# New steps for every kind of work in a planned two-stage attention kernel

## Chip, core and metric

The kernel runs on one core of a Trainium2 chip. The metric is the device time of one execution in microseconds, the median of several runs.

## What is computed

x is 8 batches of 1024 rows of 512 channels; ctx is 8 batches of 1024 rows of 384. Two stages follow each other, both in fp32:

```python
# stage 1: cross attention, 8 heads of 64
q = layernorm(x) @ Wq;  k = ctx @ Wk;  v = ctx @ Wv
x = x + tanh(g_xattn) * (softmax(q @ k.T / 8) @ v @ Wo + bo)
# stage 2: self attention, 16 heads of 32, q normalised, gated
y = layernorm(x); q, k, v = (y @ W.T + b for each)
q = (q / |q| + query_embedding) * softplus(temperature)
h = softmax(q @ k.T / sqrt(32)) @ v
gates = softmax(h @ Wr.T + br), only the best 3 of 15 kept, times 3
s = softmax(h @ Ws.T + bs); w = 2 * s
x = x + tanh(g_ffn) * ((h * (w0 * s0 + w1 * sum(gates))) @ Wp.T + bp)
```

## The kernel before

**Tiling.** A batch has 64 steps, counted on through all 16 batches of work (8 of stage 1, then 8 of stage 2). Step T is 128 keys against 512 queries of one group of heads: 2 heads in stage 1, 4 in stage 2. A batch has 4 groups of 16 steps, a half group (8 steps) shares its queries. In a step the tensor engine (PE) makes the scores of each head (kind "S", line 925), ScalarE (ACT) their exponentials ("ex", L1128) into a ring of buffers, PE the weighted values of all heads ("PV", L942), and GpSimd (POOL) adds the exponentials up ("ad", L817), for the sums of the softmax ("sm", L954, made to factors by "sma" and "ev").

**Work that fills.** Around the steps lies the work for later groups and batches. "pq" and "pk" project queries and keys of a group (L839); "sd" copies them by DMA into `stack` as high and low parts. "mx" makes all scores of a head once more (L902) and VectorE (DVE) takes their maxima ("mxr", L1286); "mt", "ml" and "md" turn these and bring them by DMA into `stack`, where the scores read them. "vp" and "vpe" project the values (L839, L1095, L1279). "xl" loads the rows of the next batch, in two halves, "ln", "la", "lb" and "l2" normalise them on DVE and ACT by turns (L1223 to L1242, L1036), "tr", "tra" and "trl" transpose them and split them in high and low (L859, L1043, L1250). "gt" and "gm" make the gates (L963), "hs", "hsl", "op", "ope" and "st" the output (L839, L1349), "xr", "xq" and "xb" bring the residual rows back. "fr" to "fs" split the weights of stage 2 during stage 1, "cx" and "cxl" the context.

**The planner.** Every instruction sequence of every engine is made from one order of about 17,000 items, made by `Plan` when the kernel is built. Each item has an engine, a time, a list of items it comes after, and a step. `Plan.run` keeps its own clock: an engine that is free takes, of the items whose predecessors are done, the one with the lowest step. The steps come from the table `AT`, one dictionary for each stage, relative to the batch: `p` and `over` the start of the four groups' projections and over how many steps they spread, `mx0` and `mxn` start and length of a group's maxima, `ctx`, `load`, `norm`, `turned` the context, the loads, the normalisations and the transposes, `out` the output of each half, `xr` the residual's load, `split` the splitting of the weights; `off` adds a number to all items of one kind. The scores of step T have step T - 1, PV has T + 0.9. The constants of the plan's clock are for instance 0.23 for a score product, 1.05 for PV, 0.52 for an exponential, 1.3 for an addition on POOL, 1.2 for a maximum on DVE; for the normalisation 3.5, 0.5, 0.8 and 3.2; a load is 0.7 on the queue and lands 6 later.

**What is fixed by it.** The order on each queue, and which of the four banks of `aux` a product gets. Each engine takes its instructions strictly in that order and waits with semaphores; the semaphores follow from the order by themselves. The transposes of a batch come, by their list `used`, behind the projections of the last group of the batch before; "S" of a group's first step comes behind "md" of its head; "sd" of the next group comes behind the last score of the group that used the same half of `stack`.

Of the kernel before, what the change touches and what calls it, by code (L numbers as in the profile page):

```python
# [37 lines left out]
class Phase:  # L38


    def __init__(self, ffn):
# [10 lines left out]
        self.SUM = 32 if ffn else 64  # L52
        self.AT = AT[ffn]
        self.first = B if ffn else 0
# [52 lines left out]
    def copied(self, g, e):  # L107
# [1 line left out]
        return g // 2 + 1 if e < PHASES[0].G else (g - NG * B) // 2 + 1  # L109


AT = (dict(p=[2.5, 18.6, 35.2, 51.9], over=7.4, mx0=3, mxn=3, ctx=[-3.6, 18.6, 24.7, 31.5], load=[5.4, 36.9], norm=[10, 28.5],
           turned=[20.8, 34.5], out=[63.1, 58.9], xr=43, split=39, off={}),
      dict(p=[2, 18.6, 36, 50], over=6.5, mx0=0.4, mxn=9, load=[4, 27], norm=[8, 29], turned=[25, 36.6], out=[61, 67], xr=49, off={}))


PHASES = Phase(False), Phase(True)
# [2 lines left out]
def stage(j):  # L120

    return PHASES[j >= B]
# [9 lines left out]
def batch(it):  # L132

    return it[1] // BATCH_HAS[it[0]] if it[0] in BATCH_HAS else 0


class Plan:
# [18 lines left out]
    def add(self, item, engine, time, step, after=()):  # L156

        assert item not in self.work, item
        self.work[item] = (engine, time, after)
        self.step[item] = step + stage(batch(item)).AT["off"].get(item[0], 0)  # L160

    def weights(self):
# [8 lines left out]
        for c in range(4 * NG):  # L171
            j, at = c // NG, c // NG * TURN + PHASES[0].AT["split"] + 3 * (c % NG)
            self.add(("fr", c), "sp", 0.7, at, [("fl", c - 2), ("tr", j + 1, 1, NG - 1)])
# [20 lines left out]
    def attend(self, j):  # L194

        ph, G = stage(j), stage(j).G
        for T in range(TURN * j, TURN * (j + 1)):
# [23 lines left out]
            if jt == TT - 1:  # L221
                b = T + 1 + ph.AT.get("sums", 0)
                self.add(("cp", h), "act", 0.6, T + 0.95, [("PV", T), ("cp", h - 1)])
# [4 lines left out]
    def project(self, g):  # L228
# [3 lines left out]
        source = lambda kind, n: ("cxl", j, 2) if kind == "pk" and not ph.ffn else ("trl", j, n, NG - 1)  # L232
        at, over = ph.AT["p"][(g + 2) % NG] + (g - 2) // NG * TURN, ph.AT["over"]
        self.add(("wl", g), "sp", 2.4, at - 3, [("pk", g - 1, 1, last_g.chunks("pk") - 1), ("pq", g - 1, 1, NG - 1)] + [("ws", i) for i in range(2)] + [("fs", 4 * NG - 1)] * ph.ffn)
# [25 lines left out]
    def maxima(self, g):  # L260

        ph = stage(g // NG)
        last_g = stage((g - 1) // NG)
        step, each = (g - 1) * STEPS + ph.AT["mx0"], ph.AT["mxn"] / ph.G
        for e in range(ph.G):
# [1127 lines left out]
```

## Time and profile before

| | us |
|---|---|
| runs | 5066.6, 5065.87, 5042.02 |
| median | 5065.87 |
| span of the profiled execution, first to last instruction | 5051.8 |
| PE / DVE / ACT / POOL busy | 94% / 58% / 51% / 67% |

The profile page gives busy time for each engine and groups of instructions by line. Records of products overlap each other: a product's record lasts longer than the time after which the next one can follow, so PE can be "busy" and still be held up. The profile has the span of one execution; its device time is not listed by itself, the median of the runs is 14.1 us more than the span.

### The profile page before, as it was taken

How to read it: one execution, taken by the hardware profiler on the slowest of the kernel's cores; microseconds unless marked ns; L12 is line 12 of the kernel's file. 1: busy time of each engine (PE TensorE's matmuls, PEld its weight loads, DVE VectorE, ACT ScalarE, POOL GpSimd, SP SyncE). 2: the span in 40 equal slices, each digit the busy share in tenths (PEclk: the TensorE clock that was granted, in tenths of full speed). 3: DMA queues.
4: the chain of work that ended last, by engine and by line, in shares of the span. 5: the costliest groups of instructions: out<-in, count | busy, mean ns of one | idle time of the engine just before them, and what ended most of it. 6: DMA issues, size and time to landing. Idle time of an engine off the chain costs nothing.

```text
span 5051.8 us, 67410 instructions
## 1 busy us (share of the span) xinstructions
PE 4766.1 (94%) x21696; PEld 2731.3 (54%) x21696; DVE 2946.6 (58%) x4019; ACT 2601.4 (51%) x4705; POOL 3367.3 (67%) x2667
## 2 busy tenths in 40 slices
PE   4999999999999999998998999999999999999997
PEld 3555555556565556564564554554654644645644
DVE  4454545454545454566766656757656666666563
ACT  2444445353535354536636646546556556466454
POOL 1656656574756565747848858767578588578587
PEclk7999999999999999999999999999999999999998
DMA  7343535344343434333233132322323322332320
GB/s 239 97 130 113 129 112 125 117 123 125 97 134 88 142 88 133 93 88 86 57 100 76 45 110 64 84 84 63 94 70 76 93 62 64 92 82 53 101 51 26
DMA packets 285210, 481.11 MB, mean 95 GB/s; under 512 B 32832, under 2 KB 165440, under 8 KB 275648
## 3 DMA queue, kind: packets, MB, share of 16 engines
q1 hardware_dynamic: 284864, 476.79, 34.6%
q8 instruction: 181, 2.97, 0.3%
q14 instruction: 165, 1.35, 0.1%
HBM read 223.14 MB, written 50.33 MB: 54 GB/s over the span
## 4 chain that ended last, share of the span: by engine, by line
PE 50%; DVE 5%; issue 3%; ACT 2%; POOL 1%; SPq 1%; DMA 0%; ACTq 0%; POOLq 0%; DVEq 0%
PE aux L839 15%; PE acc L942 10%; PE aux L902 10%; PE scores L925 9%; DVE nm L1286 4%; PE aux L954 2%; PE aux L963 1%; PE aux L883 1%; POOL added_f L817 1%; PE aux L859 1%; SPq L734 1%; ACT probs L1128 1%; DMA stack<-ck_lo 0%; PE aux L911 0%; DVE st L1223 0%
## 5 line engine op out<-in xcount | busy, mean ns | idle before, releaser
L1286 DVE TENSOR_REDUCE nm<-aux 128x1 f32<-128x1024 f32 x1536 | 1844.7, 1221 | 1192.8 <-PE aux L902 1190.0
L817 POOL TENSOR_TENSOR added<-added,probs 128x512 f32<-128x512 f32 x1433 | 1804.4, 1297 | 856.7 <-PE acc L942 653.4
L1128 ACT ACTIVATE probs<-scores 128x512 f32<-128x512 f32 x2151 | 1189.1, 597 | 862.5 <-PE scores L925 831.3
L925 PE MATMUL scores<-stack 128*128 128x512 f32 x4096 | 1340.3, 417 | 36.3 <-ACT probs L1128 15.8
L902 PE MATMUL aux<-stack 96*128 96x512 f32 (+1 forms) x3072 | 1017.5, 420 | 94.1 <-DVE nm L1286 53.6
L925 PEld LDWEIGHTS scores<-stack 128*128 128x128 f32 x4096 | 735.3, 190 | 639.2 <-ACT probs L1128 223.7
L942 PE MATMUL acc<-probs,vh 128*32 128x512 f32 (+1 forms) x4302 | 968.8, 617 | 20.0 <-ACT vh L1095 20.0
L902 PEld LDWEIGHTS aux<-stack 96*128 96x128 f32 (+1 forms) x3072 | 525.6, 190 | 578.1 <-DVE nm L1286 272.1
L817 POOL TENSOR_TENSOR added_f<-added_f,probs 128x512 f32<-128x512 f32 x537 | 678.9, 1298 | 59.1 <-PE acc L942 36.9
L839 PE MATMUL aux<-xT_hi,wqk 128*128 128x512 f32 x1536 | 580.2, 407 | 13.7 <-ACT qwork L1067 6.9
L1128 ACT ACTIVATE more<-scores 128x512 f32<-128x512 f32 x537 | 300.3, 598 | 155.6 <-PE scores L925 134.7
L804 POOL TENSOR_TENSOR cq_lo<-qwork,cq_hi 128x512 fp32r<-128x512 f32 x64 | 82.5, 1288 | 417.2 <-ACT cq_hi L1083 417.2
L839 PEld LDWEIGHTS aux<-xT_hi,wqk 128*128 128x128 f32 x1536 | 290.3, 189 | 111.7 <-issue 47.6
L942 PEld LDWEIGHTS acc<-probs,vh 128*32 128x32 f32 (+1 forms) x4302 | 156.9, 119 | 303.6 <-issue 221.8
L817 POOL TENSOR_TENSOR added_f<-added_f,more 128x512 f32<-128x512 f32 x231 | 296.0, 1308 | 31.3 <-PE acc L942 25.9
L817 POOL TENSOR_TENSOR added<-added,more 128x512 f32<-128x512 f32 x231 | 291.3, 1292 | 19.4 <-PE acc L942 18.9
L839 PE MATMUL aux<-xT_lo,wqk 128*128 128x512 f32 x768 | 302.7, 394 | 0.0
L942 PE MATMUL acc<-more,vh 128*32 128x512 f32 x1074 | 288.6, 617 | 0.0
L1309 DVE SCALAR_TENSOR_TENSOR aux<-aux,rn 128x512 f32<-128x512 f32 x128 | 88.8, 694 | 249.7 <-ACT rn L1141 234.8
L1128 ACT ACTIVATE added<-scores 128x512 f32<-128x512 f32 x256 | 143.6, 596 | 173.7 <-PE scores L925 170.3
L839 PE MATMUL aux<-wvo,halves_f 128*128 128x512 f32 x768 | 217.6, 426 | 5.9 <-DVE xs L1349 4.4
L823 POOL TENSOR_TENSOR xs<-xs,bo_x 128x512 f32<-128x512 f32 x64 | 81.6, 1289 | 161.5 <-DMA xs<-in_x 161.5
(131 smaller groups left out, 4938.1 us busy)
## 6 DMA issues: line engine op xcount, KB each, us to landing
wqk<-w_split SPq DMA_DIRECT2D x256, 256.0 KB, 3.8
wvo<-w_split SPq DMA_DIRECT2D x64, 1024.0 KB, 6.9
stack<-cq_hi SPq DMA_DIRECT2D x128, 256.0 KB, 5.0
stack<-ck_hi SPq DMA_DIRECT2D x128, 256.0 KB, 4.9
stack<-cq_hi SPq DMA_DIRECT2D x256, 128.0 KB, 2.3
stack<-ck_hi SPq DMA_DIRECT2D x256, 128.0 KB, 2.4
xs<-in_x SPq DMA_DIRECT2D x16, 1024.0 KB, 6.4
stack<-cq_lo SPq DMA_DIRECT2D x64, 256.0 KB, 4.9
```

The lines of the kernel that those rows point to most:

```text
L734: sp.dma_start(stack[row:row + D, g % 2, e * ph.SLOTS + slot, :].bitcast(F32), src[what][half][e * D:(e + 1) * D, :].bitcast(F32)).then_in ...
L804: pool.tensor_tensor(cq["lo"][:, q], qy[:, n], cq["hi"][:, q].bitcast(F32), ALU.subtract).then_inc(qlo_ok, 1)
L817: pool.tensor_tensor(onto, onto, exp_buffer(T, e), ALU.add).then_inc(added_ok, 1)
L823: pool.tensor_tensor(xs[:, t % (TT // 2), :], xs[:, t % (TT // 2), :], bo[:], ALU.add).then_inc(biased, 1)
L839: ins = pe.matmul(out, lhs(a, k), rhs(c, k), start=k == 0 and i == 0, stop=k == whole - 1 and i == 2)
L902: ins = pe.matmul(aux[:, b + j, :], stack[used, g % 2, e * ph.SLOTS + qs, t * P:(t + 1) * P], stack[used, g % 2, e * ph.SLOTS + ks, j * HA ...
L925: ins = pe.matmul(scores[:, u % SCORES, :], stack[:, g % 2, e * ph.SLOTS + ks, jt * P:(jt + 1) * P], stack[:, g % 2, e * ph.SLOTS + qs, n ...
L942: ins = pe.matmul(acc[e * D:(e + 1) * D, :], v[:, g, jt * P + e * D:jt * P + (e + 1) * D], exp_buffer(T, e), start=jt == 0, stop=jt == TT - 1)
L954: ins = pe.matmul(out[e * D:(e + 1) * D, :], ones[:, 0:ph.SUM], exp_buffer(T, e), start=i == 0, stop=i == ph.APART)
L1128: act.activation(exp_buffer(T, e), scores[:, (n - 1) % SCORES, :], ACT.Exp, scale=ph.SCALE).then_inc(probs_ok, 1)
L1286: dve.tensor_reduce(nm[:, e * TT + t:e * TT + t + 1], keys, axis=AX.X, op=ALU.max, negate=True).then_inc(emptied["dve"], 1)
L1309: link(dve.scalar_tensor_tensor(src, src, -1.0, rn[:], ALU.mult, ALU.mult))
```

## The change

The table `AT` gets other numbers, and its `off` entries, empty before, get numbers for some kinds. No instruction is added or taken away, no constant of the plan's clock and no dependency is touched. What can differ is the order of the instructions on each engine and the banks.

```diff
-AT = (dict(p=[2.5, 18.6, 35.2, 51.9], over=7.4, mx0=3, mxn=3, ctx=[-3.6, 18.6, 24.7, 31.5], load=[5.4, 36.9], norm=[10, 28.5],
-           turned=[20.8, 34.5], out=[63.1, 58.9], xr=43, split=39, off={}),
-      dict(p=[2, 18.6, 36, 50], over=6.5, mx0=0.4, mxn=9, load=[4, 27], norm=[8, 29], turned=[25, 36.6], out=[61, 67], xr=49, off={}))
+AT = (dict(p=[2.5, 18.6, 34.75, 51.9], over=11.12, mx0=4.25, mxn=2.58, ctx=[-7.05, 18.38, 25.72, 26.18], load=[6.61, 47.22], norm=[14.88, 27.21], turned=[22.82, 38.71], out=[63.1, 56.31], xr=39.87, split=48.43, off={"pkl": -0.57, "ssa": -0.17, "ad": 1.02, "mx": -0.56, "tr": -0.03, "mxr": 0.36, "ev": 0.18, "trl": 2.59}),
+      dict(p=[5.57, 19.27, 36, 50], over=7.35, mx0=0.4, mxn=7.05, load=[-7.54, 24.72], norm=[8.92, 26.32], turned=[23.04, 33.76], out=[60.35, 63.48], xr=33.59, off={"op": 0.1, "ln": 0.78, "ssa": -0.79, "hs": 0.25, "ope": -3.12, "sma": -0.35, "s2": 0.59, "hsl": -0.43, "tra": 0.4, "pqa": 0.03, "ev": 2.12}))
```

## Rows read from the trace of the kernel before

**Rows 1.** Head of the page: busy us, share, instructions; PE and clock in slices.

```profile
span 5051.8 us, 67410 instructions
PE 4766.1 (94%) x21696; PEld 2731.3 (54%) x21696; DVE 2946.6 (58%) x4019; ACT 2601.4 (51%) x4705; POOL 3367.3 (67%) x2667
```

**Rows 2.** Busy time by windows (us); columns as in the second line.

```profile
core 0: us, PE busy (x) PEld busy (x) DVE busy (x) ACT busy (x) POOL busy (x), PEclk, DMA share, GB/s
345.90:2177.70 1831.80, 1806.01 (x7364) 1037.82 (x7363) 942.26 (x1272) 839.14 (x1494) 1108.02 (x864) 1.00 0.43 115
2554.60:4685.30 2130.70, 2014.55 (x9985) 1153.61 (x9984) 1384.84 (x1920) 1231.90 (x2256) 1563.86 (x1246) 0.98 0.29 78
4685.30:5051.80 366.50, 326.18 (x1578) 180.33 (x1576) 189.75 (x255) 179.05 (x330) 261.60 (x210) 0.94 0.21 58
0.00:107.60 107.60, 39.38 (x140) 30.24 (x141) 47.43 (x102) 33.22 (x49) 19.16 (x22) 0.75 0.74 242
```

**Rows 3.** Costliest groups of the page: busy, mean ns of one | idle before.

```profile
L1286 DVE TENSOR_REDUCE nm<-aux 128x1 f32<-128x1024 f32 x1536 | 1844.7, 1221 | 1192.8 <-PE aux L902 1190.0
L817 POOL TENSOR_TENSOR added<-added,probs 128x512 f32<-128x512 f32 x1433 | 1804.4, 1297 | 856.7 <-PE acc L942 653.4
L1128 ACT ACTIVATE probs<-scores 128x512 f32<-128x512 f32 x2151 | 1189.1, 597 | 862.5 <-PE scores L925 831.3
L925 PE MATMUL scores<-stack 128*128 128x512 f32 x4096 | 1340.3, 417 | 36.3 <-ACT probs L1128 15.8
```

**Rows 4.** Chain that ended last: start us, us on the chain, what, count.

```profile
2938.75 6.82 PE aux L839 x30
...
3088.91 0.44 PE aux L859 x4
...
3089.82 1.00 PE acc L942 x8
...
3106.36 1.97 PE aux L859 x8
3108.32 0.85 PE scores L925 x2
3109.18 1.87 PE acc L942 x8
```

**Rows 5.** Waits of PE from 2260 to 5000: us in total, times, longest.

```profile
PE aux L902 <- DVE nm L1286: 48.2, 94, 6.0
PE aux L859 <- ACT xs L1036: 31.9, 7, 4.6
```

**Rows 6.** Windows counting the score products (line 925) of one batch of stage 2.

```profile
core 0: us, PE busy (x) PEld busy (x), PEclk, DMA share, GB/s
2910.00:3072.80 162.80, 35.62 (x102) 19.30 (x103) 0.98 0.32 89
2910.00:3089.30 179.30, 40.60 (x117) 21.74 (x118) 0.98 0.31 87
2910.00:3106.30 196.30, 44.86 (x128) 23.69 (x128) 0.98 0.32 89
2910.00:3275.20 365.20, 95.25 (x271) 49.87 (x271) 0.98 0.31 83
```

**Rows 7.** Timelines of SP, DVE, ACT and PE near 3100: start us, us.

```profile
3089.38 0.38 SPq L637 DMA_DIRECT2D xs<-x_after_xattn  x1
...
3104.00 0.68 SPq L741 DMA_DIRECT2D stack<-mrow  x1
...
3096.06 2.46 DVE L1223 BATCH_NORM_STATS2 st<-xs 128x6 f32<-128x512 f32 x4
...
3099.05 2.34 DVE L1286 TENSOR_REDUCE nm<-aux 128x1 f32<-128x1024 f32 x2
...
3103.26 0.27 DVE L1296 CAST mrow<-aux 8x128 fp32r<-8x128 f32 x1
...
3103.38 2.93 ACT L1036 ACTIVATE xs<-xs,rs 128x512 f32<-128x512 f32 x4 [3.05 <-DVE rs L1242]
...
3101.54 0.27 PE L911 MATMUL aux<-ident,nm 128*8 128x128 f32 x1 [0.59 <-DVE nm L1286]
3106.36 1.97 PE L859 MATMUL aux<-ident,xs 128*128 128x128 f32 x8 [4.55 <-ACT xs L1036]
```

**Rows 8.** Window around that hole.

```profile
3096.00:3110.00 14.00, 8.32 (x41) 4.34 (x37) 8.08 (x26) 8.22 (x17) 11.30 (x10) 0.79 0.52 116
```

**Rows 9.** Timeline of PE at the gate products, then a window.

```profile
3275.26 2.85 PE L963 MATMUL aux<-wg,vh 128*128 128x18 f32 x24
...
3279.08 1.73 PE L963 MATMUL aux<-wg,vh 128*128 128x18 f32 x8
...
3280.64 4.19 PE L839 MATMUL aux<-wvo,halves_f 128*128 128x512 f32 x9
...
3278.00:3286.00 8.00, 8.00 (x26) 6.66 (x27) 4.62 (x25) 0.21 (x1) 1.26 (x1) 0.57 0.30 66
```

**Rows 10.** Windows: POOL's lull, and the hole behind the value projections.

```profile
2932.00:2973.00 41.00, 39.76 (x176) 28.03 (x175) 25.89 (x47) 16.14 (x27) 8.84 (x8) 1.00 0.38 129
3014.00:3030.00 16.00, 14.03 (x63) 5.78 (x60) 2.81 (x4) 10.47 (x21) 16.00 (x14) 0.89 0.36 80
```

**Rows 11.** Waits of PE over the whole span, and PE's timeline at the start.

```profile
PE acc L942 <- ACT vh L1095: 20.0, 11, 2.8
...
84.27 2.04 PE L902 MATMUL aux<-stack 128*128 128x512 f32 x4 [23.72 <-DMA stack<-ck_lo]
```

## Prediction, made before the changed kernel was run

> **What bounds the kernel now.** I read the page first: TensorE (PE) is busy 94% of a span of 5051.8 us, GpSimd (POOL) 67%, VectorE (DVE) 58%, ScalarE (ACT) 51% [rows 1]. PE is the bound, and since the change adds and removes no instruction, time can only come from three places: PE standing still, PE working at the 1.2 GHz level, and products that are issued later than they could be but that the busy share hides. The third is real: a record of a score product lasts 417 ns, while products that are not held up follow each other every 6.82 us / 30 = 0.227 us [rows 3, 4]. So a "busy" stretch can still be slack.
>
> Second view: the windows by stage. Seven steady batches of the attention stage keep PE busy for 1806.0 of 1831.8 us (98.6%) at full clock; six steady batches of the second stage only for 2014.6 of 2130.7 us (94.6%), at a mean clock of 0.98. The first 107.6 us hold 39.4 us of PE work, the last 366.5 hold 326.2 [rows 2]. Visible standing still in the steady part is thus 25.8 us in one stage and 116.2 in the other. The second stage is where a new order can pay, at 2130.7 / 6 = 355.1 us a batch, 5.55 us for each of its 64 steps.
>
> Third view: who PE waits for there. The largest single cause that is one place and not a hundred is "PE aux L859 <- ACT xs L1036": 31.9 us in 7 waits, longest 4.6 [rows 5]. These are the transposes of the second half of the next batch's normalised rows: once in each of the seven batches of that stage that have a successor. The second cause, DVE's maxima (L1286), is 48.2 us in 94 waits, spread out.
>
> **The hole at the half of a batch, followed.** The scores issued since step 0 of a batch are counted: 4 a step. With the one issued before the window opens, the projection of the fourth group ends near score 103 (step 25.7), the first half's transposes near score 118 (step 29.5), and the second half's start at score 129 (step 32.2) [rows 6]. Between the last two runs one serial chain [rows 7]: the load of xs is issued at 3089.38, the statistics start at 3096.06 (6.7 us), two maxima of the batch's last head lie in the middle of the normalisation on DVE, ACT's four scalings start at 3103.38 after ACT waited 3.05 us, and PE's transposes start at 3106.36 after it stood still 4.55 us. That is 17.0 us from load to transposes. The plan's constants make of it 0.7 + 6 for the load and 3.5 + 0.5 + 0.8 + 3.2 for the arithmetic, 14.7 us and short lags; the program order made with them therefore puts the transposes where the data is some us late. The clock then drops: 0.79 over the 14 us around it, and behind the hole the same eight accumulating products take 1.87 us and not 1.00, the eight transposes 1.97 us and not 2 x 0.44 [rows 4, 8]; that is 0.87 + 1.09 = 2.0 us. The hole costs 4.6 + 2.0 = 6.6 us, seven times.
>
> **What the change does, part by part.** In this planner a step is no start time. It is a rank: an engine that is free takes, of what is ready, what has the lowest step (the scores of step T have rank T - 1). So a step later than the readiness of an item matters, and a step earlier only matters among things that are ready together.
>
> (a) Transposes of the second stage (turned 25 to 23.04, load 27 to 24.72, norm 29 to 26.32 with +0.78 on "ln"). The first half's transposes cannot start before the fourth group's projections are out, since these read the same tile (the `used` list). The projections now run from 19.27 over 7.35 steps and end at 26.6, where they ended at 18.6 + 6.5 = 25.1: 1.5 steps later. But the transposes (old ranks 25, 26, 27, 28, one a step; new 23.04 to 26.04) will by then all be overdue and follow each other at once. Seen end was step 29.5; new end 25.7 + 1.5 + up to 1 step for four = 28.2 at the latest, and with a bank wait more 28.7. So the load is issued 0.8 to 1.3 steps sooner, at (3089.3 - 3072.8) x 4 / 15 = 4.4 us a step here [rows 6] 3.5 to 5.7 us. I take 4.3 of the 4.6 us as gone, and with it the slow clock: 6.3 x 7 = 44 us. What is late next is the row of maxima of the last head, which S of step 32 needs: its transpose stands at 3101.5, its copy to SBUF only at 3103.26 behind the normalisation, its DMA at 3104.00 [rows 7]. If that wait takes over, about 3 us a batch remain won and the part gives 21 us. Bounds: 0 (the transposes land late again) to 6.6 x 7 = 46.
>
> (b) Output of the second stage (out 61, 67 to 60.35, 63.48; +2.12 on "ev", -3.12 on "ope"). The second half's gate products were ranked 65.5 and came at 3275.26, step 67 to 68 [rows 6, 9]; they are now due as soon as the sums of step 64 are normalised, about 1.5 steps sooner. Those steps last 4 us each, so the output block and the value projections behind it come some 6 us sooner. What follows them is bound by POOL: in 3014 to 3030 POOL is busy 16.00 of 16 us and PE, "busy" 14.03, issues only 36 of PV's products at 8 in 1.00 us, 20 scores and 6 for maxima at 0.23, 10.5 us in all [rows 4, 10]. POOL ran out of work before: 8.84 us busy of the 41 us from 2932 to 2973 [rows 10]. A POOL that starts 6 us sooner takes up to 16 - 10.5 = 5.5 us out of that hole, in 8 batches 0 to 44 us. I take half, 22 us, because POOL's adds of a batch start only behind the value projections, whose weights have their own load in between.
>
> (c) Maxima (window 9 to 7.05 steps in the second stage, 3 to 2.58 with mx0 later by 1.25 in the first). A group has 32 reductions of 1221 ns, 39.1 us on DVE [rows 3], which is 7.05 x 5.55 = 39.1 us: the new window asks DVE for all of its time. But in the trace the maxima already run late of their ranks (the two last reductions start at 3099.05 [rows 7], near step 31, and are ranked before 16 + 9.4 = 25.4), so DVE and the banks set their pace and not the rank. Where they do come sooner, by up to 2 steps, the steps behind them have only scores and PV (0.92 + 1.00 us a step) under ACT's 4 x 0.597 = 2.39 us or POOL's 4 x 1.297 = 5.19 us [rows 3]: 0.9 to 6.5 us a group. I take 0.5 us for 31 groups, -15 us; bounds 0 to -60, or +5 where DVE's better packing shortens a wait.
>
> (d) First stage (over 7.4 to 11.12, ctx, load 36.9 to 47.22, turned, split, xr). Its transposes come about 3.7 steps later (18.6 + 11.12 in place of 18.6 + 7.4), its last load with them; the user of the result, the projection of half 1 of the next group, is ranked 34.75 + 5.56 = 40.3, and 17 us of chain are 4 steps, so it is covered: step 30 + 4 = 34. The stall that is seen, PV behind ACT's copy of the values, is 20.0 us in 11 waits [rows 11], and the rank of the value projections is not touched. I take 0; bounds -10 to +15 us.
>
> (e) The start. Steps of batch 0 are negative ranks; the second load of x falls from -27.1 to -16.8, behind the constants (-30) and the first weights on SP's queue. PE waits there anyway 23.72 us for the copies to the stack [rows 11]. 0; bounds 0 to -6, once.
>
> **The sum.** 5051.8 - 44 - 22 + 15 = 5000.8 us of span. The median of the runs is 5065.87, 14.1 us above the profiled span, and I keep this distance: 5015 us, 1.0% less. One of the three runs is at 5042, so a single kernel moves by 0.5% by itself; 0.5% (25 us) is what I call a difference.
>
> **A rule against the change.** The gate products are 18 columns wide; 24 of them take 2.85 us, and the next 8, with PE never idle, 1.73 us, the nine output products behind them 4.19 us where 2.04 is their full pace; the clock in 3278 to 3286 is 0.57 [rows 9]. So here the clock fell without a hole. The Trainium skill ("TensorE: Matmul & The Clock Gate", "The HAM clock gate") states that the throttled clock is the default and activity releases it, which fits. The new ranks put four gate groups directly behind each other, where a maximum and a score lay between the third and the fourth; by that rule the drop stays at least as it is, and no gain in (b) may be booked from the clock.
>
> **The rivals.**
> 1. The holes close further: all of (a), all of (b), and (c) gives its 5 us: 5065.9 - 46 - 44 - 5 = 4971. For it: all batches of a stage have one pattern, so what a new order wins it wins seven or eight times. Against it: the maxima stay bound by DVE.
> 2. Nothing measurable. The plan's clock closes holes that its own clock sees; the one at the half batch is there because of what this clock has wrong. If the order again puts the transposes a constant distance behind a chain that is counted 2 us short, the hole moves with it and (b) is eaten by (c): 5055, between 5041 and 5080.
> 3. Slower. The denser maxima take PE and both bank pairs in the first half of each group and leave the second half bare. Price 2 steps x (2.39 - 1.92) = 0.9 us to 2 x (5.19 - 1.92) = 6.5 us a group; at 3.5 us, the middle, 31 x 3.5 = 108, less the 44 of (a): 5130; at 2.2 us 5090. It decides from 44 / 31 = 1.4 us a group on. For it: a search that drives every item to the edge of readiness on the plan's clock leaves no slack for waits of the kind of those 48.2 us [rows 5], and all queues are in order. Against it: the maxima lag their ranks already.
>
> **How the numbers follow.** Forecast (sum) 0.42, with its own range 4990 to 5040; rival 1 0.16; rival 2 0.24; rival 3 0.18. Faster by over 0.5% takes the forecast nearly whole and rival 1: 0.56; within 0.5%: rival 2 and the edges 0.26; slower 0.18. The range reaches down into rival 1 and up over rival 2 into the near part of rival 3: 4955 to 5088.
>
> **What would show it.** Right: the waits of L859 on ACT xs in the second stage under 10 us in total, no slow clock at step 32, a batch of about 348 us in place of 355.1, the attention stage within 5 us of 262 a batch, POOL's idle stretch around step 4 shorter. Wrong: the 7 waits of 4.6 us still there (rival 2), "PE aux L902 <- DVE nm" grown well over 48 us or PE less busy at steps 8 to 16 of each group (rival 3), or a start longer than 107.6 us. A move of the attention stage by over 20 us in either sense would mean that (d), which I put at nothing, was the term that mattered.

## The result

The changed kernel takes 5137.07 us (median of 4 runs), the kernel before 5066.24 (4 runs): 1.014 times as long, 95% interval 1.011 to 1.017. The forecast was 5015, its range ended at 5088, and the sign was wrong. Head of the profile page of the changed kernel (its lines of code have numbers one lower than before):

```profile
span 5139.8 us, 67404 instructions
PE 4796.9 (93%) x21696; PEld 2746.9 (53%) x21696; DVE 2977.1 (58%) x4019; ACT 2595.5 (50%) x4705; POOL 3368.6 (66%) x2667
```

The profiled execution took 5141.55 us, only 1.8 more than its span. The distance of 14.1 us that the prediction added to its sum was therefore no cost around the span; the profiled execution of the kernel before was simply a shorter one than its median.

The windows by stage, cut where the same batches begin (batch 1 to 8, batch 9 to 15, the rest, the start), answer to [rows 2]:

```profile
core 0: us, PE busy (x) PEld busy (x) DVE busy (x) ACT busy (x) POOL busy (x), PEclk, DMA share, GB/s
350.30:2236.00 1885.70, 1823.46 (x7367) 1044.36 (x7366) 946.29 (x1274) 838.18 (x1494) 1108.25 (x862) 0.99 0.42 113
2622.20:4779.90 2157.70, 2022.70 (x9987) 1159.27 (x9983) 1415.37 (x1919) 1226.98 (x2256) 1564.64 (x1248) 0.97 0.28 77
4779.90:5139.80 359.90, 321.60 (x1569) 179.99 (x1565) 178.42 (x253) 178.71 (x330) 258.71 (x207) 0.94 0.21 58
0.00:112.00 112.00, 41.72 (x155) 32.32 (x155) 49.98 (x104) 34.01 (x50) 19.17 (x22) 0.85 0.77 246
```

Against [rows 2] the seven batches of stage 1 are 1885.7 - 1831.8 = 53.9 us longer, the six of stage 2 2157.7 - 2130.7 = 27.0, the start 4.4, the end 6.6 shorter; the first batch of stage 2, between the windows, is 386.2 against 376.8. That is 53.9 + 27.0 + 4.4 - 6.6 + 9.4 = 88.1 us, the whole difference of the spans. The stage that the prediction put at nothing lost most. Against the forecast of 5000.8 us for the span the measured one is 139 us longer: 54 us of it in stage 1, 81 in stage 2 (a gain of 51 was forecast, a loss of 30 came), 4 at the start.

Waits of PE in the changed kernel (us in total, times, longest), first in stage 2 (2330 to 5070), then in the steady part of stage 1 (345 to 2230):

```profile
PE aux L901 <- DVE nm L1285: 79.3, 88, 10.5
PE aux L901 <- DMA stack<-ck_lo: 37.2, 15, 4.0
```

```profile
PE aux L901 <- DMA stack<-ck_lo: 29.9, 10, 5.7
```

and the second cause in the same stretches of the kernel before, 2260 to 5000 and 345 to 2170:

```profile
PE aux L902 <- DMA stack<-ck_lo: 8.5, 9, 1.6
```

```profile
PE aux L902 <- DMA stack<-ck_lo: 5.8, 4, 1.7
```

The seven stops of the transposes [rows 5] have gone from the list, as forecast. In their place stand the copies of queries and keys to `stack`, in both stages, and a longest wait of 10.5 us behind a maximum, which was 6.0. There are three waits of 10.5 us, 31.5 of the 79.3 us; without them, and without the one of 6.0 before, this cause stands at 48 us where it was at 42.

Two scenes explain these lines. The first is stage 1 near step 36. Timeline of SP and of PE in the changed kernel:

```profile
1035.08 2.59 SPq L699 DMA_DIRECT2D wqk<-w_split  x4
1039.49 0.34 SPq L624 DMA_DIRECT2D raw<-in_ctxT  x1
1040.12 0.39 SPq L636 DMA_DIRECT2D xs<-in_x  x1
1042.21 0.54 SPq L733 DMA_DIRECT2D stack<-cq_hi  x1
...
1055.61 0.70 PE L901 MATMUL aux<-stack 128*128 128x512 f32 x2 [3.06 <-DMA stack<-ck_lo]
```

and in the kernel before:

```profile
1011.41 0.34 SPq L625 DMA_DIRECT2D raw<-in_ctxT  x1
1013.07 0.39 SPq L637 DMA_DIRECT2D xs<-in_x  x1
...
1019.50 0.55 SPq L734 DMA_DIRECT2D stack<-cq_hi  x1
...
1029.67 1.15 PE L902 MATMUL aux<-stack 128*128 128x512 f32 x4 [1.67 <-DMA stack<-ck_lo]
```

The loads that follow the end of the projections now start 2 to 3 us ahead of the first copy, where they started 6 to 8 us ahead. From the first copy's issue to the first product for the maxima it is 13.4 us and was 10.2.

The second scene is the end of a batch of stage 2. DVE and POOL of the changed kernel, then windows with PE's share:

```profile
2595.29 12.65 DVE L1301 TENSOR_TENSOR halves_f<-vh,halves_f 128x512 fp32r<-128x512 f32 x1
...
2591.33 3.77 POOL L816 TENSOR_TENSOR added_f<-added_f,more 128x512 f32<-128x512 f32 x3
2595.06 8.67 POOL L816 TENSOR_TENSOR added_f<-added_f,probs 128x512 f32<-128x512 f32 x7
2603.69 3.70 POOL L816 TENSOR_TENSOR added_f<-added_f,more 128x512 f32<-128x512 f32 x3
```

```profile
2596.00:2609.00 13.00, 2.70 (x12) 1.87 (x10) 13.00 (x3) 2.41 (x5) 11.39 (x10) 0.80 0.06 21
2609.00:2620.00 11.00, 10.78 (x40) 6.99 (x41) 6.19 (x7) 1.89 (x4) 2.56 (x2) 0.78 0.28 95
```

A subtraction on DVE (the low part of an output tile) has a record of 12.65 us. It begins 0.2 us behind the start of an addition in the middle of a run on POOL; this one and nine more follow each other without a gap, and it ends 0.5 us after the last of them. The maximum that PE waits for stands behind it on DVE: PE works 2.7 of the 13 us and comes back at a mean clock of 0.78. All instances of that line, in the changed kernel and in the kernel before:

```profile
L1301 DVE TENSOR_TENSOR halves_f<-vh,halves_f x64: 668/682/12649, 2581.4 to 5128.1; 128x512 fp32r<-128x512 f32 x64
```

```profile
L1302 DVE TENSOR_TENSOR halves_f<-vh,halves_f x64: 669/682/10747, 2520.5 to 5040.1; 128x512 fp32r<-128x512 f32 x64
```

(minimum, median and maximum in ns). The median is 0.68 us. The kernel before had two of over 5 us, the changed one three of 12.6. I call them long subtractions below. They do not come wherever a subtraction meets the additions. Three batches of the changed kernel have a case like this one:

```profile
3328.86 1.60 DVE L1301 TENSOR_TENSOR halves_f<-vh,halves_f 128x512 fp32r<-128x512 f32 x1
...
3327.37 4.24 POOL L816 TENSOR_TENSOR added_f<-added_f,more 128x512 f32<-128x512 f32 x3
```

Here, too, the subtraction begins 0.2 us behind the start of an addition, but it is done after 1.60 us, about the wait for that one addition, and the three additions on POOL take 4.24 us in place of 3.77. What decides between the two outcomes is not shown.

### The profile page after: what moved, and what is told of

Read it like the earlier page. It is cut to its first block, busy times and chain, and to the rows that moved or that the text cites. A ratio compares the mean times of both kernels' runs of the same rounds, so it can differ in the third digit from the quotient of the medians.

```text
span 5139.8 us, 67404 instructions
## 1 busy us (share of the span) xinstructions
PE 4796.9 (93%) x21696; PEld 2746.9 (53%) x21696; DVE 2977.1 (58%) x4019; ACT 2595.5 (50%) x4705; POOL 3368.6 (66%) x2667
## 4 chain that ended last, share of the span: by engine, by line
PE 49%; issue 4%; DVE 3%; ACT 1%; SPq 1%; DMA 1%; POOL 1%; ACTq 0%; POOLq 0%; DVEq 0%
PE aux L838 14%; PE aux L901 10%; PE acc L941 10%; PE scores L924 9%; DVE nm L1285 2%; PE aux L953 2%; PE aux L962 1%; SPq L733 1%; DMA stack<-ck_lo 1%; PE aux L882 1%; POOL added_f L816 1%; PE aux L858 1%; ACT probs L1127 0%; PE aux L910 0%; ACT more L1127 0%
## 5 line engine op out<-in xcount | busy, mean ns | idle before, releaser
L901 PE MATMUL aux<-stack 96*128 96x512 f32 (+1 forms) x3072 | 1034.6, 426 | 192.1 <-DMA stack<-ck_lo 92.8
```

The lines of the kernel that those rows point to most:

```text
L901: ins = pe.matmul(aux[:, b + j, :], stack[used, g % 2, e * ph.SLOTS + qs, t * P:(t + 1) * P], stack[used, g % 2, e * ph.SLOTS + ks, j * HA ...
```

## The experiments

Each is run with the kernel before on the same chip, and the ratio is to that. The kernel before took 5054.8 to 5075.2 us beside them, so the ratios are to be compared and not the medians. "x" of a name is stage 1, "f" stage 2. The table lists all; batches are the time between the first scores of neighbouring batches in the one profiled execution, for batches 1 to 6 of stage 1 and 9 to 14, of stage 2; undisturbed are those without a long subtraction.

| run | median us | ratio (95%) | batches of stage 1 | of stage 2, undisturbed | long subtractions (over 5 us) |
|---|---|---|---|---|---|
| before | 5066.24 | 1 | 260 to 262 | 352 to 359 | 2 |
| after | 5137.07 | 1.0142 (1.0114, 1.0170) | 265 to 271 | 355 to 358 | 3 |
| x_new | 5111.53 | 1.0102 (1.0053, 1.0151) | 266 to 270 | as before | 2 |
| f_new | 5119.21 | 1.0104 (1.0073, 1.0135) | as before | 358.6 | 4 |
| x_over | 5153.60 | 1.0200 (1.0124, 1.0276) | 267 to 279 | as before | 2 |
| f_turn | 5079.52 | 1.0045 (1.0019, 1.0071) | as before | 355 | 5 |
| x_over_small | 5074.48 | 0.9995 (0.9969, 1.0021) | 256 to 263 | as before | 2 |
| f_new_pool | 5064.09 | 0.9990 (0.9966, 1.0014) | as before | 354 to 363 | 0 |
| f_out | 5070.05 | 1.0006 (0.9991, 1.0022) | as before | 356 to 363 | 0 |
| f_mxn9 | 5139.80 | 1.0137 (1.0104, 1.0170) | as before | none | 7 |
| x_over_late | 5212.67 | 1.0269 (1.0243, 1.0295) | 276 to 282 | as before | 3 |
| after_cured | 5178.54 | 1.0187 (1.0152, 1.0223) | 274 to 281 | 354 to 362 | 0 |
| best2 | 5190.19 | 1.0220 (1.0196, 1.0245) | 274 to 282 | 352 to 362 | 0 |
| best3 | 5193.66 | 1.0226 (1.0206, 1.0246) | 274 to 287 | 354 to 360 | 0 |
| f_turn_pool | 5041.73 | 0.9974 (0.9963, 0.9985) | as before | 352 to 360 | 0 |
| after_pool | 5119.44 | 1.0121 (1.0101, 1.0140) | 266 to 269 | 357 to 362 | 0 |
| f_mxn9_pool | 5051.74 | 0.9988 (0.9969, 1.0006) | as before | 351 to 360 | 0 |
| x_over_wqk | 5109.64 | 1.0113 (1.0084, 1.0142) | 262 to 274 | as before | 2 |

### The two stages apart

x_new has the new dictionary of stage 1 and the old one of stage 2, f_new the reverse.

> Stage 1 has the new steps, stage 2 the old ones. In the profile of the changed kernel a batch of stage 1 is some 6.5 us longer than before, a batch of stage 2 some 3 us. Theory A (the loss of stage 1 belongs to its own steps): 5066 + 7 x 6.5 = about 5112 us, 5100 to 5125, with the waits of L901 on the copies to the stack at step 36 of every batch, and stage 2 back at 355 us a batch. Rival B (stage 1 loses because work of the two stages shares queues only at the change of stage, or by chance of alignment): within 15 us of 5066.

> Stage 1 has the old steps, stage 2 the new ones. Theory A: 5066 + 25 = about 5090 us (5075 to 5105), with the three stalls of over 10 us behind an output product. Rival B: the new steps of stage 2 gain when left alone (the prediction's sum gave -51) and the loss seen in stage 2 is brought over from stage 1: 5015 to 5050. If A holds, the losses of this run and of x_new add up to the 71 us of the whole change, to 15 us.

Stage 1's loss belongs to its own steps: 1.0% of 5066 is 52 us. f_new lost 53 us, more than expected, and its batches split in two kinds: 358.6 us where no subtraction was long, 365 to 371 where one was. The two do not add up to the 71 us of the whole (105). The count of long subtractions (2, 4 and 3) differs from order to order, so parts of this change need not be additive.

### One number of stage 1

```diff
-AT = (dict(p=[2.5, 18.6, 35.2, 51.9], over=7.4, ...
+AT = (dict(p=[2.5, 18.6, 35.2, 51.9], over=11.12, ...
```

> The kernel before with one number changed: over of stage 1 from 7.4 to 11.12. Theory A: the projections that end 3.7 steps later push the reload of the projection's weights, the context and the rows up against the copies to the stack, and that is most of stage 1's loss: 5095 us, 5085 to 5112, stage 1 at 266 us a batch. Rival C: the loss comes from the later maxima (mx0) or the output block (out, xr, split), and this run is within 10 us of 5066.

1.0200: this number alone costs 94 us against the runs beside it, more than all new steps of stage 1 together (the intervals overlap; batches 1 to 7 take 1918 us in the profile, 1884 in x_new, 1832 before). Waits of PE in x_over:

```profile
PE aux L901 <- DMA stack<-ck_lo: 97.0, 26, 23.9
```

23.9 of it is the start. The other new numbers of stage 1, then, win back some 40 to 50 us of what `over` loses; which of them does was not tried.

x_over_small keeps every instruction in its place and takes bytes from two loads ahead of the copies: the weights of the projections bring a quarter, the rows for the normalisation an eighth. The residual rows stay whole. x_over_wqk takes bytes from the weights alone.

```diff
-  sp.dma_start(xs[:], rows(...)).then_inc(...)
+  few = slice(0, DM // 8 if 0 < j < B else DM)
+  sp.dma_start(xs[:, :, few], rows(...)[:, :, few]).then_inc(...)
...
-  sp.dma_start(wqk[:, what, part].bitcast(F32), w_split[...][:, :, ...]).then_inc(w_loaded, 16)
+  few = slice(0, 1) if 0 < g < NG * B else slice(0, NG)
+  sp.dma_start(wqk[:, what, part, few].bitcast(F32), w_split[...][:, few, ...]).then_inc(w_loaded, 16)
```

> x_over (over of stage 1 at 11.12, all else old) with smaller loads in the same places: the weights of the projections of stage 1 bring an eighth of the columns' blocks asked for (one of four k blocks), the rows of batches 1 to 7 an eighth of their channels, so that the results of stage 1 are wrong; every instruction and its place in its queue stays. Theory A (the copies to the stack are slow because some 2 MB of loads are on the same DMA engines just ahead of them): from the last score of the old half to the first maximum of the new group 15.4 us (step 36) and 19.4 us (step 52) in x_over fall to 10.5 to 12 us, and the time from 5154 to 5080 to 5110 us. Rival D (the time lies in the issue of the copies on SP's queue, or in the later end of the projections, not in the bytes): 5145 to 5160.

> x_over with only the projection's weights of stage 1 made small (one of four k blocks, stage 1's results are wrong); rows and context whole. If the weights, issued 5 to 7 us before the copies, are the load that slows them: the first maximum comes 12 to 13 us after the last score and the time is 5075 to 5100. If it is the rows, issued 1 us before: 15 to 16 us, and 5125 to 5150.

Mean time from the last score of the old half of `stack` to the first maximum of the new group, at step 32 and at step 48 of a batch: before 10.9 and 11.3 us, after 15.8 and 12.4 (its maxima are also ranked later, but PE waits for the copies there), x_over 15.9 and 16.5, x_over_small 12.3 and 14.4, x_over_wqk 14.8 and 14.3. The time goes from 1.0200 to 0.9995 with both loads small and to 1.0113 with the weights alone. So it is the bytes, not the places in the queues or the later projections; weights and rows share it, and the weights alone neither free the copies as far as expected nor leave them as slow as in the other case. The means at step 48 hide two kinds of batches. In batches 0 to 3 the residual rows (four loads of 256 KB) are issued just ahead of the copies, in the later ones nine steps earlier. x_over has 18.4 to 19.4 us in the former and 12.4 to 14.2 in the latter, x_over_small 15.6 to 17.7 and 11.7. At step 32 of batch 7, where the loads are those of stage 2 and whole, x_over_small has 18.3 us against 11.4 to 11.5 in batches 1 to 6. The copies are slow where whole loads are left ahead of them. One reserve: the kernel before was not run with the small loads, and these may also help elsewhere in stage 1, whose batches fall to 256 us, below those of the kernel before.

Then the same bytes in another order: the plan puts these loads behind the copies.

```diff
-  self.add(("wl", g), "sp", 2.4, at - 3, [...])
+  self.add(("wl", g), "sp", 2.4, at - 3, [...] + [("sd", g - 1, last_head)] * (not ph.ffn))
```

and likewise for "xl" of the second parts and for "xr".

> x_over with the same bytes, but the plan now puts the loads of stage 1 that stood just ahead of the copies to the stack (the projection's weights, the last third of the context, the second half of the rows, the residual rows) behind them. Theory A (loads ahead of the copies slow them): the step from the last score of the old half to the first maximum falls from 15.9 and 16.5 us (groups 3 and 0 of a batch) to about 11, and the time from 5154 to 5050 to 5090 us. The plan's own clock says the opposite, 22 us more than for x_over, 5175; a rival that the later projections themselves cost the time gives 5140 to 5160.

A miss that teaches. The copies became quick (12.1 and 11.7 us), as theory A says, and the kernel got the highest ratio of all (its interval just meets x_over's), while the next user of a load now waits. Waits of PE in x_over_late and, from its timeline, one of them:

```profile
PE aux L838 <- DMA wqk<-w_split: 78.1, 30, 7.4
```

```profile
948.68 0.80 PE L838 MATMUL aux<-xT_hi,wqk 128*128 128x512 f32 x1 [4.25 <-DMA wqk<-w_split]
```

My reading, not tried by itself: with the projections spread over 11 of 16 steps there is no place left between the end of one group's projections and the start of the next's in which both the weights and the copies travel unhindered; the kernel before had that place because its projections ended earlier. Three kernels that combine this order with other parts show the same 274 to 287 us in stage 1 and miss their expectations with it. after_cured has it under all new steps, best2 under part (a) of stage 2, best3 under all new steps of stage 2, each with the low parts of stage 2 made by POOL (below):

> The changed kernel with both cures: loads of stage 1 planned behind the copies to the stack, and the low part of stage 2's output tiles made by POOL. If the two contentions (the copies behind loads, the DVE subtraction held off by POOL) are the whole loss, the 71 us come back and part of the plan's gain with them: 5137 - 45 (stage 1) - 3 x 12 (long subtractions) = 5056, 5035 to 5070. If something else in the new steps costs as much: above 5085.

> Both cures, over of stage 1 at 11.12, and of stage 2 only the steps of part (a) (p, over, load, norm, turned). Sum: x_over_small's stage 1 batches were 257 us against 261, f_turn's batches without a long subtraction 355: 5066 - 7 x 3 - 10 = 5035, 5015 to 5060. If moving the subtraction to POOL costs what the plan's clock says (2.4 us a batch of stage 2): 5055.

> Both cures, over of stage 1 at 11.12, stage 2 with all the new steps as in f_new_pool (5064, its batches 358 us). Sum: 5064 - 7 x 3 = 5043, 5025 to 5060; against best2 it tells whether the rest of the new steps of stage 2 (maxima, out, off) gain or lose on the chip once the long subtractions are gone: the plan's clock has them 2.4 us a batch better than best2, f_new against f_turn had them 3.5 us a batch worse.

All three have higher ratios than the changed kernel (after_cured's interval overlaps), and the batches of stage 1 account for it; none has a long subtraction in stage 2.

### The long subtraction

In f_new_pool the subtraction is an instruction of POOL, so that it stands in one queue with the additions.

```diff
-  self.add(("hsl", t), "dve", 0.7, ...)
+  self.add(("hsl", t), "pool" if ph.ffn else "dve", 1.3 if ph.ffn else 0.7, ...)
...
+  pool.wait_ge(h_hi_ok, t + 1)
+  pool.tensor_tensor(lo, outputs(t), hi.bitcast(F32), ALU.subtract).then_inc(h_lo_f, 1)
```

> f_new (stage 2 with the new steps, stage 1 old) with the subtraction that makes the low part of an output tile in stage 2 (halves_f) moved from DVE to POOL, planned and waited for there; the plan's order shifts with it. Theory E (a DVE subtraction with both operands in SBUF cannot start while POOL's additions follow each other, which made it 12.65 us long instead of 1.09 in four of eight batches of f_new, each time with PE still for over 10 us): no DVE instruction longer than 4 us is left, no batch over 362 us, and 5119 falls by 4 x 11 = 44 to 5060 to 5085. Rival F (the long record is only a wait of DVE for something else that comes late there, for instance ACT's copy): PE still stands for 10 us at that place in some batches, 5105 to 5125.

The instruction now takes 1.26 to 1.31 us in all 64 instances, no batch has the stop, and the ratio falls from 1.0104 to 0.9990, 58 us for four long subtractions. (The 1.09 us of the expectation is a mean that long ones are part of; the median is 0.68. And one batch, at 363 us, is over its limit of 362.) The pair f_mxn9 and f_mxn9_pool repeats it with seven:

> f_new with the maxima spread over 9 steps again instead of 7.05: part (c) undone. The prediction's third rival put the denser maxima at 0.9 to 6.5 us a group, 28 to 200 us; then this run is at 5119 - 28 or lower, 5090 or less. If the window of the maxima is not what costs: 5105 to 5130. The plan's clock makes it 17 us slower than f_new, which would be 5136.

> f_new_pool (5064) with the maxima spread over 9 steps again. f_mxn9 had a long subtraction in all seven batches from the first of stage 2 on and was 5140; if that is all that made it slow, 5140 - 7 x 11 = 5063, 5045 to 5075, and the width of the maxima's window is worth less than 10 us either way. If the window itself costs, 5080 or more (wider is worse) or 5040 or less (denser was worse).

1.0137 to 0.9988, 75 us for seven, 10.8 us each. The line in f_mxn9:

```profile
L1301 DVE TENSOR_TENSOR halves_f<-vh,halves_f x64: 669/682/12923, 2521.4 to 5112.1; 128x512 fp32r<-128x512 f32 x64
```

In the changed kernel itself:

> The changed kernel with stage 2's low parts made by POOL and nothing else. Three long subtractions go: 5137 - 3 x 12 = 5101, 5085 to 5115; what is left over 5066 is then stage 1's, 52 us by x_new, less what the batches of f_new_pool give. If the long subtractions only stand where PE would have waited anyway: 5125 to 5145.

Only 11 us came back (1.0142 to 1.0121), not 36, and as the intervals overlap not even these are certain. The record of three long ones is of one execution, and the plan's order for POOL's version is another one, with batches of 357 to 362; so for the changed kernel I can say that this is a part of stage 2's loss, not that it is all of it.

### The parts of the prediction alone

> The kernel before with p, over, load, norm and turned of stage 2 from the change, all else old: part (a) of the prediction alone. Part (a) as predicted: the seven stops of 4.6 us before the second half's transposes go and 21 to 46 us are gained, 5020 to 5045 us. Rival: the stops go, but PE then waits for the copies to the stack for the first maxima of the next group at the same step 32, as it does in the changed kernel: 5055 to 5075.

> f_turn (part (a) alone) with stage 2's low parts made by POOL. best2 had the same stage 2 and batches of 352 to 355 us but for one, against 355 before and 355 to 369 in f_turn. If part (a) is worth what its undisturbed batches show: 5066 - 7 x 2 - 10 (the two long subtractions of the kernel before) = 5042, 5030 to 5055. If the transposes' stop is only replaced by the wait for the copies: 5058 to 5075.

f_turn (p, over, load, norm, turned of stage 2) has no stop of the transposes in stage 2 either, yet is 0.45% slower: five of its subtractions are long. f_turn_pool has none and is 0.26% (0.15 to 0.37), 13 us, faster than the kernel before, the only one here whose interval lies below 1. But these 13 us are not part (a)'s alone. The kernel before has two long subtractions, which at 10.8 us each could be worth 21 us, and no run has the old steps with the subtraction on POOL. The profile puts the gain where these two stand: the first batch of stage 2 is 358.9 us against 376.8, the last 362.2 against 366.5. The six batches between, which have no long subtraction in either kernel, are not shorter (2130.70 us in [rows 2]):

```profile
2540.00:4673.80 2133.80, 2005.64 (x9985) 1158.22 (x9984) 1356.19 (x1873) 1232.10 (x2256) 1615.77 (x1300) 0.97 0.29 78
```

Where the 44 us went, from the waits of its stage 2 (2330 to 5036) and its timeline at step 32 of a batch:

```profile
PE aux L906 <- DMA stack<-ck_lo: 39.3, 21, 4.1
```

```profile
3452.09 1.17 PE L906 MATMUL aux<-stack 96*128 96x512 f32 x4 [2.67 <-DMA stack<-ck_lo]
```

Against 8.5 us in 9 waits before: 30.8 us more, where the stops of the transposes had been 31.9. The transposes no longer stand at step 32, and the first maxima of the next group, whose copies can only start behind the last score of step 31, stand there instead.

Part (a) said that the stops would go because the load of the second half's rows is issued sooner. It is not. The changed kernel in the batch that the prediction followed, its first score at 2986.4: SP's load and PE's first transposes of the second half, then windows counting score products up to the end of the projections, to this load and to these transposes, as in [rows 6]:

```profile
3171.44 0.38 SPq L636 DMA_DIRECT2D xs<-x_after_xattn  x1
...
3188.38 0.60 PE L858 MATMUL aux<-ident,xs 128*128 128x128 f32 x4
```

```profile
2986.40:3163.30 176.90, 38.42 (x115) 21.16 (x116) 0.98 0.29 81
2986.40:3171.40 185.00, 42.02 (x124) 22.75 (x124) 0.98 0.30 83
2986.40:3188.40 202.00, 47.16 (x137) 25.64 (x137) 0.97 0.34 94
```

The projections end at step 28.8 in place of 26 (the prediction read 25.7), the load is issued at step 31.0 in place of 29.5, and the transposes stand at 34.2 in place of 32.2, still 17 us behind the load. PE does not wait for them because two steps of other work now lie ahead of them. In f_turn and f_turn_pool the load comes at step 29.8 and the transposes at 34.0.

> The kernel before with out of stage 2 from [61, 67] to [60.35, 63.48] and nothing else: part (b) of the prediction alone, which was put at -22 us (0 to -44). The plan's own clock gives it -20 us. If part (b) was right: 5022 to 5050. Rival: as for the other parts the plan's gain does not arrive, 5055 to 5075, with the long DVE subtraction in other batches than before or more of them.

Part (b) brings nothing: 1.0006 (0.9991 to 1.0022), although f_out has no long subtraction and the kernel before has two. Its six batches 9 to 14 are longer in the profile, 2152.1 us against 2130.7 (one execution each). Windows from 50 to 60 us behind the first score of batch 10, in the kernel before and in f_out, and in f_out also from 80 to 90 us:

```profile
2959.30:2969.30 10.00, 10.00 (x51) 6.42 (x50) 7.82 (x26) 3.71 (x8) 3.85 (x4) 1.00 0.55 157
```

```profile
2956.20:2966.20 10.00, 10.00 (x53) 5.45 (x52) 4.70 (x5) 5.13 (x9) 10.00 (x9) 1.00 0.01 2
2986.20:2996.20 10.00, 10.00 (x48) 5.81 (x46) 7.05 (x8) 5.52 (x11) 0.00 (x0) 1.00 0.54 211
```

POOL does start sooner, as forecast (10.00 us busy in place of 3.85), and then stands still for 13.3 us waiting for the weighted values of PE; before, its longest stop in that stretch was 5.4 us.

## Why the prediction was wrong, point by point

**The kind of error.** The sum had one term that was left out, one that was put at nothing and is the largest, and two gains that did not come.

**(d), stage 1, put at 0 with bounds -10 to +15: +52 us.** This is the step that failed. The text checked whether the late transposes are in time for PE (they are), and then stopped. It named the moved loads but did not ask what transfers they now travel with. What the runs show in its place: loads issued just ahead of the copies to `stack` slow these, and PE waits for them. The window in [rows 2] even gave the DMA engines' busy share in stage 1, 0.43 against 0.29 in stage 2. The prediction's own sign for this error, stage 1 moved by over 20 us, came: 53.9. Shown: x_new, x_over, x_over_small. Not shown: how the 52 us split between waits for copies (29.9 - 5.8 = 24 us in the steady part), the slower clock (0.99 over that part, and 1.00 before) and the rest.

**The missing term: a DVE instruction held off by POOL.** The kernel before had two of them, one of 8.4 us beside a stop of PE. They were in its trace and not in the prediction, since the instances of that line, 0.68 us in the median and 10.7 at most, were not read one by one. Shown by the two pairs with and without POOL. For the changed kernel itself it is three waits of 10.5 us in its profile, and after_pool did not give them back clearly.

**(a), -44 us: a second step that failed.** The stops went, but not in the way forecast: the load was to be issued 0.8 to 1.3 steps sooner and is issued 1.5 steps later, because the projections end 2.8 steps later and not 1.5, and the transposes come two steps later. The waits for the copies of the new group took over what the stops had cost (30.8 for 31.9 us in f_turn_pool). The part is worth at most the 13 us of f_turn_pool and, by its six steady batches, nothing; the share of the two long subtractions in the 13 us was not measured. The prediction said that something else may be late next and gave 21 us for that case; it named the row of maxima of the old group, and it was the copies for the new one. The sign that the waits of L859 fall under 10 us came true and was thus no proof of the gain.

**(b), -22 us: 0.** POOL's start was brought forward as forecast, but without profit: the time came back as a stand of POOL behind PE. What holds the batch there was not tried further.

**(c), +15 us** (its paragraph writes the loss as -15, the sum adds it). By the run times no difference between the windows of 7.05 and 9 steps can be told: 0.9990 and 0.9988 once POOL makes the low parts. In the profiles of these two the six batches 9 to 14 take 2150.7 and 2132.9 us and the last one 360.3 and 372.6, so a loss of up to 3 us a batch by the denser window is not ruled out. The third rival, slower through denser maxima, had the right sign and, with 5090 to 5130, nearly the size, by luck: its sign, PE's waits behind the maxima grown from 48.2 to 79.3 us, is there, but 31.5 of the 79.3 are the three waits behind long subtractions. In f_mxn9 the wider window was even the slower one, with seven long subtractions against four.

**(e), the start: +4.4 us** of the 6 that were its bound.

**Rival 2** told half of the story: a hole that moves. It expected the same transposes to be late again; the hole moved to the next late thing instead.

**The rule on the clock** expected the drop behind the gate products to stay at least as it was, and no gain from the clock was booked; that caution cost nothing. The drop itself did not stay: the gate products stand in one row of 32, as forecast, and the 8 us that begin 2.7 us behind their first have a mean clock of 0.79 in the same batch, where they had 0.57 [rows 9]:

```profile
3353.60:3361.60 8.00, 7.42 (x28) 5.43 (x27) 5.04 (x26) 2.25 (x5) 1.27 (x1) 0.79 0.77 181
```

The mean granted clock of the whole span fell all the same, from 0.977 to 0.971, so the time at 1.2 GHz rose from about 2 x 0.023 x 5051.8 = 232 us to 2 x 0.029 x 5139.8 = 298 us; at most half of the 66 us, 33 us, is time lost by it (an estimate).

**The plan's own clock**, as each kernel's planner computes it, was run over these kernels afterwards: 4845.8 us for the kernel before, 4753.0 for the changed one, a gain of 92.8 us that became a loss of 88 in the span. For x_over it has 4839.9, for x_over_late 4861.6, for f_mxn9 4777.1. Of these it had only x_over_late on the right side of the kernel before; for f_turn_pool (4812.7) it had the sign, and 33 us where 13 arrived. The plan's clock holds durations, order and banks. Two things that the runs above show to matter it does not hold: copies have a fixed time whatever else is on the DMA engines, and DVE's time does not depend on POOL.

## What to carry to other kernels

When an order is searched on a model's clock, the gain is paid in what the model leaves out, so first list the contentions (transfers beside transfers, engines that hold each other off) and see in the trace where the present order happens to avoid them; a later end of a phase moves its follow-up loads into the next phase's transfers. Open every group whose mean lies well above its usual instance before a reorder: one long instance per batch is a hazard whose count changes with any order. And a closed stop is worth only the distance to what is late next: here 31.9 us of stops went and 30.8 us of waits for copies came.

## What the runs showed of the hardware

A DVE tensor_tensor with both inputs in SBUF, 0.68 us in the median, had a record of 12.65 us while ten additions of 1.25 us on SBUF ran on POOL one behind the other; up to 12.92 us in other orders. All 21 records of over 5 us in before, after, f_new, f_turn and f_mxn9 end 0.55 us behind the last addition of the run. Moved to POOL it took 1.28 us. The Trainium skill ("SBUF — State Buffer", "SBUF: two separate sides" and "Who interferes with whom") says that such an instruction contends with a POOL instruction that reads SBUF and that the one that starts first holds the shared ports for its whole instruction; the contention agrees. By that rule the wait would be one addition, 1.25 us, and that is what the subtractions of 1.60 to 1.63 us in three batches of the changed kernel look like. The long ones wait through ten, as if a queue of ready POOL instructions had no gap for them; that this is the mechanism is inferred from where the records begin and end, and why it happens in some batches only is open.

Copies inside SBUF (q and k to `stack`, 256 KB each): in batch 3 of stage 1 the first product that needs them came 10.2 us behind the issue of the first copy when 2.5 MB of loads (weights, context, rows) had been issued 6 to 14 us ahead of it, and 13.4 us when the same loads had been issued 2 to 7 us ahead. At step 48 the way from the last score to the first maximum, 11.3 us before, was 18.4 to 19.4 us in x_over in the batches with the residual rows (1 MB, issued 2 us ahead) among the loads, and 12.4 to 14.2 in those without.
